# Eight-head attention: VectorE clips and masks one exponential tile in four, in the place of TensorE's mask matmul

## What is computed

```
scores = einsum('bhnd,bhmd->bhnm', q, k) / sqrt(16)
scores = where(adjacency == 0, -inf, scores)
w      = softmax(scores, axis=-1)
out    = einsum('bhnm,bhmd->bhnd', w, v) @ Wo.T + bo
```

## Time and profile before

| what | value |
|---|---|
| three runs, median (lowest to highest) | 5080.75 us (5075.43 to 5083.6) |
| profiled execution: device time, span | 5091.8 us, 5090.0 us |
| busy share of the span | TensorE 72%, VectorE 57%, ScalarE 40%, GpSimd 33% |
| mean granted TensorE clock | 0.81 |
| turned scores of the two attention stages start | 105.5 to 2438.4 us, with the LSTM between them |
| mask matmuls (L1208) | 1024, of which 898 were recorded |

### The profile page before, as it was taken

The page is one execution under the profiler, slowest core; times in us unless marked ns, Lnnn a source line. Parts: engine busy times, 40 slices in busy tenths (PEclk is TensorE's granted clock), DMA queues, the critical chain, the costliest instruction groups (busy, mean ns, idle before and its releaser), DMA issues. The chain is left out here.

```text
span 5090.0 us, 82513 instructions
## 1 busy us (share of the span) xinstructions
PE 3668.9 (72%) x24079; PEld 2253.2 (44%) x24205; DVE 2893.1 (57%) x11117; ACT 2018.5 (40%) x5054; POOL 1698.5 (33%) x1934
## 2 busy tenths in 40 slices
PE   3999975666666389999868666299575677773995
PEld 1333324444444233333555555166464344442663
DVE  5666654555555666666578765322477555553444
ACT  1666642222222156666322455143265343331221
POOL 3444511000000154543541123634423333333444
PEclk9999985555555599999989787599788898885997
DMA  4333329100000133332000121144431000001445
GB/s 130 116 101 106 104 101 419 70 0 0 0 0 0 48 116 113 100 101 66 5 1 0 51 67 43 43 143 141 137 107 34 1 9 13 14 12 48 124 131 159
DMA packets 237329, 378.20 MB, mean 74 GB/s; under 512 B 24832, under 2 KB 157056, under 8 KB 228672
## 3 DMA queue, kind: packets, MB, share of 16 engines
q1 hardware_dynamic: 218688, 337.44, 20.9%
q0 software_dynamic: 18432, 38.31, 2.2%
HBM read 210.70 MB, written 164.95 MB: 74 GB/s over the span
## 5 line engine op out<-in xcount | busy, mean ns | idle before, releaser
L1427 DVE CUSTOM_DVE_ANT_0 mha_seen<-mha_score,mha_mask 128x512 f32<-128x512 f32 x1024 | 686.4, 688 | 455.3 <-PE mha_score L1198 452.3
L1330 ACT ACTIVATE mha_prob<-mha_turned 128x512 f32<-128x512 f32 x1024 | 609.0, 601 | 489.7 <-PE mha_turned L1209 459.5
L1591 PE MATMUL lstm_gates<-lstm_h_part,lstm_w_part 128*128 128x16 f16 x4608 | 277.5, 179 | 337.4 <-DVE lstm_h_part L1778 337.4
L1198 PE MATMUL mha_score<-mha_k_rows,mha_q_rows 96*128 96x512 bf16 x1024 | 397.1, 390 | 56.3 <-DMA mha_k_rows<-split_rows 28.1
L3295 POOL DMA_INDIRECT expert_rows<-expert_y,expert_target x320 | 307.6, 961 | 376.3 <-DVE expert_y L3441 155.3
L1591 PEld LDWEIGHTS lstm_gates<-lstm_h_part,lstm_w_part 128*128 128x128 f16 x4608 | 215.9, 107 | 483.3 <-DVE lstm_h_part L1778 481.4
L1209 PE MATMUL mha_turned<-mha_q_rows,mha_k_rows 99*128 99x512 bf16 x1024 | 390.5, 381 | 14.6 <-issue 9.9
L1208 PE MATMUL mha_turned<-mha_maskT,core_ident_bf 128*128 128x512 bf16 x898 | 343.6, 383 | 3.8 <-ACT mha_prob L1330 3.5
L1541 POOL TENSOR_TENSOR core_mid<-lstm_hist,lstm_per_unit 128x128 f32 x64 | 29.5, 461 | 875.6 <-DVE lstm_hist L1779 875.6
L878 DVE CUSTOM_DVE_ANT_0 mha_prob<-mha_score,mha_mask 128x384 f32<-128x384 f32 (+3 forms) x256 | 124.9, 488 | 306.6 <-PE mha_score L517 224.0
L689 ACT ACTIVATE mha_prob<-mha_prob,mha_bias 128x384 f32<-128x384 f32 (+3 forms) x256 | 143.5, 561 | 362.5 <-DVE mha_bias L878 355.8
(11 more groups left out here) (564 smaller groups left out, 9010.0 us busy)
## 6 DMA issues: line engine op xcount, KB each, us to landing
routed_rows<-lstm_blank SPq DMA_DIRECT2D x66, 1056.0 KB, 27.1
core_params<-adj SPq DMA_DIRECT2D x32, 1024.0 KB, 5.7
gat_adj_raw<-adj SPq DMA_DIRECT2D x32, 1024.0 KB, 5.3
mha_q_rows<-split_rows SPq DMA_DIRECT2D x64, 384.0 KB, 4.4
mha_k_rows<-split_rows SPq DMA_DIRECT2D x64, 384.0 KB, 5.3
expert_x<-routed_rows SPq DMA_DIRECT2D x80, 264.0 KB
expert_w<-weights SPq DMA_DIRECT2D x80, 256.0 KB
combine_pair<-expert_rows SPq DMA_DIRECT2D x32, 512.0 KB, 4.6
```

The costliest lines, as they stand in the source:

```text
L1198: pe.matmul(score[n % 2][:, :], rows[0][s][0:ROWS, h, t * P:(t + 1) * P], rows[1][s][0:ROWS, h, :], start=True, stop=True).then_inc(S["sco ...
L1330: act.activation(prob[:, n % RING, :], turned[n % 2][:, :], ACT.Exp, scale=-1.0).then_inc(S["prob_ready"], 1)
L1427: dve.tensor_tensor_reduce(seen[n % 2][:, :], score[n % 2][:, :], mask[1 - s][:, t, :], 1.0, 3e38, ALU.add, ALU.min, low[g][:, t, j:j + 1] ...
L1591: return pe.matmul(out, w[:, g * P:(g + 1) * P], h_part[:, part, :], start=False, stop=stop, skip_group_check=True)
```

## The change

In every fourth item (n%4 = 3, the last of each quad) the mask matmul is left out, and the product alone starts and ends the bank. ScalarE's exponential of that item is then of unmasked scores, and can overflow. VectorE makes good for both in place: `shut` takes the minimum with 3e38 and multiplies by `allowed`, a table of 1 for a neighbour and 0 otherwise, in one scalar_tensor_tensor over the 128x512 f32 tile. `allow` makes the table from `maskT` once per graph (128x2048 in bf16, two buffers), at n=30 of the period before. `shut` of quad n//4 - 1 stands in VectorE's list behind the `seen` pass of n = 5, 9, ..., 29, that of the last quad at n=1 of the next period, ahead of `take_rows`. The values group waits for `shut` in the place of `prob_ready`. The other three items of a quad are as they were.

```diff
@@ attn_stage
+        allowed = [m.sb(f"allowed{s}", [P, T, N], BF16) for s in range(2)]
@@ tensor: scores_turned
                 need(pe, "prob_ready", ITEMS * b + n - 1)
-                pe.matmul(turned[n % 2][:, :], core.ident_bf[:, :], maskT[s][:, u, :], start=True, stop=False)
+                if n % 4 < 3:
+                    pe.matmul(turned[n % 2][:, :], core.ident_bf[:, :], maskT[s][:, u, :], start=True, stop=False)
                 pe.matmul(turned[n % 2][:, :], rows[1][s][0:ROWS + 3, h, u * P:(u + 1) * P], rows[0][s][0:ROWS + 3, h, :],
-                          start=False, stop=True).then_inc(S["turned_done"], 1)
+                          start=n % 4 == 3, stop=True).then_inc(S["turned_done"], 1)
@@ tensor: values
-                need(pe, "prob_ready", ITEMS * b + 4 * quad + 4)
+                need(pe, "shut", 8 * b + quad + 1)
@@ vector
+            def allow(x, s):
+                need(dve, "maskT_ready", 2 * x + 2)
+                need(dve, "shut", 8 * (x - 1))
+                dve.tensor_scalar(allowed[s][:, :, :], maskT[s][:, :, :], 0.0, None, ALU.is_equal).then_inc(S["allowed_set"], 1)
+
+            def shut(x, s, quad):
+                tile = prob[:, (4 * quad + 3) % RING, :]
+                need(dve, "allowed_set", x + 1)
+                need(dve, "prob_ready", ITEMS * x + 4 * quad + 4)
+                dve.scalar_tensor_tensor(tile, tile, 3e38, allowed[s][:, quad % 4, :], ALU.min, ALU.mult).then_inc(S["shut"], 1)
@@ vector: period, after the seen pass of item n
+                    if n == 1 and tail:
+                        shut(b - 1, 1 - s, 7)
+                    if n % 4 == 1 and n > 4 and has_t:
+                        shut(b, s, n // 4 - 1)
                     if n == 1 and prep:
                         take_rows(b + 2, s)
@@ vector: period, at its end
+                    if n == 30 and has_s:
+                        allow(b + 1, 1 - s)
```

More of the change, by code:

```diff
@@ L971, in attn_stage @@
                  "v_done", "v_ready", "oT_ready", "back_done", "ctx_chain", "ctx_ready", "ctxt_in_psum", "ctxT_ready", "attn_done",
-                 "base_chain", "base_ready", "out_taken", "tail", "saved"]
+                 "base_chain", "base_ready", "out_taken", "tail", "saved", "allowed_set", "shut"]
         S = {n: m.sem(n) for n in names}
```

## The result

The changed kernel takes 5345.62 us (median of 4 runs, 5330.02 to 5354.43); the kernel before, run beside it, 5082.18 us (4 runs, 5075.43 to 5093.94). The ratio is 1.0511, with a 95% interval of 1.0493 to 1.0529: 263 us slower. The forecast was 5408 in a range of 5290 to 5520.

A forecast was written before the change was run, and what follows sets the result against it. TensorE's instruction order was taken to set the pace. New wait 193 - removed matmuls 53 + GpSimd hold 139 + clock 48 = +327 us, taking the median from 5080.75 to about 5408 us, range 5290 to 5520.

The forecast's parts named there:

- Term 1: TensorE in both attention stages: 8 mask matmuls fewer per period, 0.22 us each, 53 us saved.
- Term 2: Values groups wait for `shut`, late in VectorE's list: 6.44 us a period, +193 us.
- the slips: Delay of each quad's values group, starting no earlier than `seen`(n-1) + 1.36 us: 0.39 to 1.65 us, none at n=18.
- Term 3: At n=9, GpSimd's `forbid` holds `shut` (two SBUF inputs) until `forbid` ends: 5.85 and 4.1 us per period, +139 us.
- Term 4: TensorE's clock falls to 1.2 GHz behind the hold of `shut`: 1.7 us each, +48 us (0 to 98).
- Rival C: TensorE's clock falls also in ordinary gaps of about 1 us: +140 us, 5548 us; chance 0.06.
- within 0.2: At n=21 `shut` slips between two of GpSimd's 1.04 us normalising operations, costing at most 0.2 us.
- A: `shut` at n=9 isn't held by GpSimd: +140 us, 5221 us; chance 0.09.
- B: TensorE's occupancy rules and the values groups' new wait is hidden: -53 us, 5028 us; chance 0.03.
- D: The change costs nothing, as TensorE's present waits for exponentials absorb the values groups' delays; chance 0.02.

The follow-up runs named there:

- drop_only: Kernel before, with every fourth item's mask matmul left out and nothing in its place (those items unmasked): 4914.38 us, ratio 0.9892 to the kernel before.
- one_input: Changed kernel with `shut` replaced by an equally long bn_stats with one SBUF input, no clip or mask: both attention stages 1390.4 us, against 1499.1 in the changed kernel.
- wait_only: Changed kernel with `shut` replaced by a memset of a spare 128x1 tile, keeping the wait without clip and mask: 5111.35 us, ratio 1.0029 to the kernel before.
- early3: Changed kernel with each `shut` two items earlier, behind the `seen` of the clipped item itself: 5125.92 us, ratio 1.0062 to the kernel before.
- early0_more: Changed kernel with `shut` one item earlier, `forbid` in four pieces, and items 5, 9, 16 also left to VectorE: 4951.04 us, ratio 0.9966 to the kernel before.
- forbid4: Changed kernel with GpSimd's mask operation `forbid` cut into four instructions of 128x512: 5263.11 us, ratio 1.0323 to the kernel before.
- forbid2: Changed kernel with GpSimd's mask operation `forbid` cut into two instructions of 128x1024: 5266.57 us, ratio 1.0345 to the kernel before.
- early0: Changed kernel with each `shut` one item earlier in VectorE's list: 5071.2 us, ratio 0.9945 to the kernel before; measured again, 4942.55 us, ratio 0.9948.

## Why the prediction was right

The direction and three of the four terms held; one term was too large. Where a term has no run of its own, it is the difference of two.

**Term 1, the removed matmuls: -53 predicted.** drop_only measures -52.1 us in the two stages and -53.8 in the median. A matmul's place in the pipe, not its duration in a row, was the right price.

**Term 2, the new wait: +193 predicted.** one_input less drop_only is 1390.4 - 1183.4 = 207.0 us. Some 16.3 of these are low clock: in 5 periods of its first stage and 7 of the second the quad 14→18 takes 6.5 to 7.1 us instead of 5.51. The rest is 190.7. wait_only splits it: 73 us are VectorE's place in the order, the other 117 its 0.69 us of work. Each of the eight quads of one_input is within 0.01 us of what the slips read off, less 0.22, make it.

**Term 3, GpSimd holds VectorE: +139 predicted.** That it would hold was right, in the place and at the time foreseen: once a period, at n=9, 1.20 us after `forbid`'s start (1.1 foreseen). Its size was not. 6→10 is 10.17 - 7.01 = 3.16 us longer than in one_input, and in the second stage 9.19 - 7.01 = 2.18: 14 x (3.16 + 2.18) = 75 us (74.6 added up), 64 less than predicted. The step that failed is the reading of the earlier trace rows, "the end of the held one follows POOL's end, whatever its length". Here it doesn't. In the first stage each of the held ones ends 5.06 us after `forbid`'s start, 2.04 ahead of its end; in the second, where `forbid` takes 5.37, it ends some 4.2 after the start, 1.2 ahead of the end:

```profile
2115.85 5.37 POOL L1090 TENSOR_SCALAR mha_mask<-core_params 128x2048 bf16<-128x2048 int32 x1
```

```profile
2117.17 2.86 DVE L1406 SCALAR_TENSOR_TENSOR mha_prob<-mha_prob,mha_allowed 128x512 f32<-128x512 f32 x1
```

That the two kinds differ is seen in early3, where one kernel has both: f32 tensor_tensors hold `shut` to their end, as in the earlier trace rows, and `forbid`, which turns int32 into bf16, lets it go before. A bf16 output alone isn't it: a tensor_tensor of GpSimd from f32 to bf16 (L1084) also held `shut` until 0.55 us behind its end in early0_more. And the part that holds is neither the instruction less a fixed stretch nor a fixed share of it. Estimated as the end of the held one less 0.55 us, the hold ended 4.5 us into 7.10 and 3.6 into 5.37 (128x2048), at the latest 1.3 into 3.65 (128x1024), and 0.6 into 1.92 and into 1.48 (128x512). What sets that point stays open.
The Trainium skill ("SBUF — State Buffer", section on the two separate sides) has the hold last for the whole instruction. By that 139 us were due and 75 were measured, so the measurement decides against that part of it. Its condition, two SBUF inputs on VectorE, is confirmed by one_input, and by `seen` with its PSUM input.

**Term 4, the clock: +48 predicted.** The quad behind the hold, 10→14, is 7.97 - 6.21 = 1.76 us longer than in one_input in the first stage and 7.22 - 6.21 = 1.01 in the second, by the medians; added up over all periods it is 37.6 us. In the first stage the clock was low 16 times (85.3 us in all), once behind each of the 14 holds and twice elsewhere; in the second 11 times, behind 9 of the 14 holds and twice elsewhere. A part of a long fall passes in the hold itself, as the prediction allowed. Rival C had falls behind ordinary gaps too, at 140 us; one_input and forbid4 show such falls, some 16 us in one_input.

**The sum.** In the two stages -52.1 + 190.7 + 74.6 + 37.6 = 250.8 of 263.6 us. Of the other 12.8, 7.2 are 18→22: there `shut` takes 0.77 to 0.88 us beside GpSimd's normalising, as the prediction's "within 0.2" had it, but which it counted at nothing, and 1.3 to 1.7 us in five periods, where it meets the start of a tensor_tensor. 5.3 are further falls of the clock, in 14→18 and 22→26. With 75 for 139 the prediction's own sum is 5408 - 64 = 5344, and 5345.62 was measured. That this is so close is luck: terms 2 and 4 were 2 and 10 us too large and what it had not counted 13, which cancel.

**The rivals.** A (no hold, 5221) is what one_input, forbid2 and forbid4 are: ratios of 1.0297 to 1.0345 on 5080.75 are 5232 to 5256, with the falls of the clock that A did not have. B (hidden, 5028) needed VectorE earlier by about one item; early0 makes just that and reaches 5053 (0.9945 x 5080.75), with half of the gain. D (no cost) is out.

## What to carry to other kernels

When a matmul group is made to wait for another engine, price the wait by that engine's place in its own in-order list, not by the work added alone: here an operation of 0.06 us in the same place cost over a third of what one of 0.69 did, and moving one call by one item was worth 5.4%, of which one item further lost 1.2% again. Before an operation with two SBUF inputs is put on VectorE, look up which long GpSimd instruction runs at that moment; cutting that one into pieces took 1.8% off. Look at the margins too: early0 escapes the hold by starting 0.2 us ahead of GpSimd's instruction, and where it started 0.43 us behind, it was held for 3.9 us. A removed 512-column bf16 matmul is worth 0.22 us where its neighbours are pipelined, and nothing where the end of a hold sets the time, and a replacement that takes 0.69 us elsewhere only pays where it lies in that engine's slack.

## What the runs showed of the hardware

- A GpSimd tensor_scalar from int32 to bf16 of 128x2048 (7.10 us with two operations, 5.37 with one) holds a VectorE operation with two SBUF inputs, but not to its end: held ones end 5.06 or 4.19 us after its start (2.04 or 1.2 ahead of its end), always at the same point, wherever between 0.43 and 3.6 us they came. One that came at 4.91 us was free.
- A piece of 128x1024 (3.65 us) did not hold what came 1.14 us in. Pieces of 128x512 (1.92 and 1.48 us) held what came 0.04 to 0.2 us in until 1.15 us after their start, and did not hold what came at 1.1 to 1.3 us.
- f32 tensor_tensors of 1.04 to 1.2 us held to their end: the held one ended 0.54 or 0.55 us behind it.
- If VectorE is first by 0.21 us, GpSimd's instruction is the one that is late: 7.44 us for 7.10.
- A bn_stats with one SBUF input took 0.690 us in the same stretch as alone.
- In stages that were otherwise busy the granted clock fell to 0.50, the 1.2 GHz level, behind waits of TensorE of some 4.0 us (14 of 14 in the first stage of the changed kernel), of 3.0 us (9 of 14 in the second) and of 1.6 us (12 to 15 of 28 in one_input, forbid2 and forbid4), and was back within 7 us. With waits of up to 1.3 us in wait_only it stayed at 1.00.
